# Another order of VectorE's instructions, and gathers released by free slots, in a graph network's edge loop

## The chip, the cores and the metric

One core of one Trainium2 chip. The metric is the device time of one execution in microseconds.

## The reference

A graph of 6250 nodes with 32 features and 106250 edges (`src`, `dst`, sorted by `dst`). Three layers of graph attention with 8 heads, each followed by a residual and a batch norm; then one message layer over the same edges. What one attention layer computes:

```python
xl = (x @ Wl + bl).reshape(n, H, C)
xr = (x @ Wr + br).reshape(n, H, C)
e = leaky_relu(xl[src] + xr[dst], 0.2)
logits = einsum('ehc,hc->eh', e, att)
m = segment_max(logits, dst)
p = exp(logits - m[dst])
denom = segment_sum(p, dst)
alpha = p / (denom[dst] + 1e-16)
out = segment_sum(xl[src] * alpha[:, :, None], dst).mean(axis=1) + bias
```

The message layer gathers features by `src`, forms a radial weight per edge, mixes, and adds the messages at `dst`.

## The kernel before, in words

Edges are laid out in steps of 256 (two to a partition), 480 steps a layer, so arranged that all edges of a step end in one block of 128 nodes; `brow` holds the block's number of each step. A layer is ten groups of 48 steps; a group is eight bodies of six steps (`S6`), the first and the last body written out, the six between them in a hardware loop on each engine. The layers and the groups 1 to 9 are hardware loops too.

A step k goes through the engines like this:

- GpSimd (L473 to L492) copies the indices of three steps (L478), then for each step issues two indirect gathers of the neighbours' rows (L490), 128 rows each, into slot k mod 6 of `xg`. Before a step it waits for `front_done` (L482) and `xs_done` (L483), that is until TensorE and ScalarE have read the slot's previous content, of step k-6. In addition the first gather waits for `oht_done` (L486), VectorE's one-hot of step k-3, and the second for `r_done` (L488), VectorE's reduction of step k-8. `then()` (L461) increments `passed`, which nobody waits for.
- SyncE loads the local destinations `dr`, three steps at a time (L410).
- VectorE makes a one-hot of the destinations (`one_hot_t`, L1139), five steps ahead. TensorE turns the gathered rows and adds the destination's rows (`front`, L597 and L600), four steps ahead; ScalarE copies the result to SBUF (`keep`, L807) and the plain rows to `xs` (L808), three steps ahead; TensorE makes the scores (`zed`, L609 and L611), two steps ahead, into one of two PSUM places; VectorE weights them (`weighted`, L1144) and reduces over channels (`over_channels`, L1152), and ScalarE copies the linear part (`linear`, L816). Every three steps VectorE writes logits (L1158).
- After a group its maxima per destination are found (`maxima`, one long chain over the engines, with L1277 near its end), and the logits are exponentiated.
- Beside group g, the weights of group g-1 are used: VectorE multiplies the rows by them (`weigh_rows`, L1171), TensorE sums over the edges with another one-hot from ScalarE (`aggregate`, L624), and VectorE adds the result to the accumulator of the step's block (`add_sums`, L1182), two steps later. For that it loads the block's number from `brow` into a register (L1178). The aggregation of k waits for the product of k and the sum of k-2 (L620, L622).

Group 0 has no aggregation beside it, and a last drain group (g = 10) has only the aggregation. A self-loop stage, the layer's output and the batch norm follow. After three layers comes the message layer (from L1383 for VectorE), which has a loop and gathers of its own (L513).

VectorE's order in a step is written out in `dve_body` (L1184): sum of k-2, product of k, logits where due, one-hot of k+5, weighting of k, reduction of k. The queues of an engine work in order; the semaphores count up over the whole kernel.

Of the kernel before, what the change touches and what calls it, by code (L numbers as in the profile page):

```python
# [38 lines left out]
S6 = 6  # L39
# [34 lines left out]
def gatv2_program(nc, x, src, dst, edge_w, edge_v, Wl, bl, Wr, br, att, conv_bias, gamma, beta,  # L74
# [3 lines left out]
    with ctx:  # L78
# [364 lines left out]
        def _(pool):  # L443
# [23 lines left out]
            with pool.Fori(0, LAYERS) as l:  # L467
# [5 lines left out]
                with pool.Fori(0, GROUPS) as g:  # L473
                    with pool.Fori(0, BODIES // 2) as i:
                        k0 = (g * BODIES + i * 2) * S6
                        for a in range(0, 2 * S6, 3):

                            nc.gpsimd.tensor_copy(idx[:, a:a + 3, :], srci[:, bass.ds(k0 + a, 3), :]).then_inc(idx_done, 1)  # L478
                            pool.wait_ge(idx_done, AHEAD + ((l * GROUPS + g) * BODIES + i * 2) * 2 + a // 3 + 1)
                            for s in range(a, a + 3):  # L480

                                pool.wait_ge(front_done, AHEAD + l * ZS + k0 + s + 1 - S6)  # L482
                                pool.wait_ge(xs_done, AHEAD + l * NS + k0 + s + 1 - S6)  # L483
                                for t in range(2):
                                    if t == 0:
                                        pool.wait_ge(oht_done, AHEAD + l * NS + k0 + s + 1 - 3)  # L486
                                    else:
                                        pool.wait_ge(r_done, AHEAD + l * ZS + k0 + s + 1 - 8)  # L488
                                    then()
                                    nc.gpsimd.indirect_dma_start(  # L490
                                        out=xg[:, s % S6, t, 96:128], out_offset=None, in_=table,
                                        in_offset=bass.IndirectOffsetOnAxis(ap=idx[:, s, t:t + 1], axis=0)).then_inc(gat[s % S6], 16)  # L492
# [481 lines left out]
        def _(v):  # L974
# [199 lines left out]
                    pg[:, 2 * j:2 * j + 2, bass.ds(c, 1), :].rearrange("p e o h -> p e (o h)").unsqueeze(3).to_broadcast([P, 2, H, C1]),  # L1174
                    ALU.mult).then_inc(px_done, 1)

            def add_sums(l, g, k, r):
                b = v.value_load(brow[0:1, bass.ds(k, 1)], min_val=0, max_val=BLOCKS - 1)  # L1178
                v.wait_ge(agg_done, AHEAD + l * NS + k + 1)
                v.wait_ge(acc_done, AHEAD + l * AGGS + 2 + g + k)  # L1180
                sums = acc[:, bass.ds(b, 1), :].rearrange("p o a -> p (o a)")
                op.tensor_tensor(sums, sums, agg_ps(r), ALU.add).then_inc(acc_done, 1)  # L1182

            def dve_body(l, g, i, a, b, starts_group, ends_group):  # L1184
                k0 = (g * BODIES + i) * S6
                for s in range(S6):
                    r = s % 2
                    if b and (s > 1 or not starts_group):
                        add_sums(l, g - 1, k0 - GS + s - 2, r)
                    if b:  # L1190
                        weigh_rows(l, g - 1, i, k0 - GS + s, s)
                    if a and s == J:
                        chunk_logits(l, g, i, 0)
                    if a and s == 0 and not starts_group:
                        chunk_logits(l, g, i - 1, 1)
                    if a and (s + 5 < S6 or not ends_group):
                        one_hot_t(l, g, i, k0 + s + 5, s + 5)
                    if a:
                        weighted(l, k0 + s, r)
                        over_channels(l, k0 + s, r, (g * BODIES + i) * 2 + s // J, s // J, s % J)  # L1200

            def dve_group(l, g, a, b):
# [4 lines left out]
                if a:  # L1207
                    chunk_logits(l, g, BODIES - 1, 1)
                if b:
                    add_sums(l, g - 1, g * GS - 2, 0)  # L1210
                    add_sums(l, g - 1, g * GS - 1, 1)

            def early_places(l, g, steps):
                for s in steps:
# [342 lines left out]
```

## Time and profile before

| | us |
|---|---|
| median of 3 runs | 9670.92 (9669.8 to 9671.51) |
| profiled execution | 9705.39 |
| its span, first to last instruction | 9703.5 |
| mean granted TensorE clock | 0.758 |

The profile is of one execution. Its page lists busy time by engine and the costliest groups of instructions; the timelines give start and duration of single instructions in us from the span's start, with the idle time of the engine before one and what ended it in brackets. DVE is VectorE, PE TensorE, ACT ScalarE, POOL GpSimd; a q behind the name is the engine's sequencer, which handles registers, loads and waits. "issue" as a releaser means that the engine waited for nothing the profile shows.

### The profile page before, as it was taken

The numbers are of one execution on the slowest core, as the hardware profiler recorded it, in microseconds if no ns is written. First come the engines' busy times: TensorE is split into PE (matmuls) and PEld (weight loads), VectorE is DVE, ScalarE is ACT, GpSimd is POOL, SyncE is SP. The second block draws the span as 40 slices with busy tenths as digits, with TensorE's granted clock in tenths as the row PEclk, the third lists the DMA queues.
The fourth block names the chain that finished last, engine by engine and source line by source line (L and its number), as shares of the span: only waits on it lengthen the run. The fifth ranks groups of instructions, "written<-read, shape, count | busy, mean of one in ns | idle before, by whom it ended". The sixth has DMA issues, their size and how long they took to land. (4 is left out here: it accounts for less than half of the span.)

```text
span 9703.5 us, 180857 instructions
## 1 busy us (share of the span) xinstructions
PE 6644.2 (68%) x27124; PEld 4815.8 (50%) x27125; DVE 7465.0 (77%) x15346; ACT 3973.6 (41%) x14623; POOL 5056.5 (52%) x5548
## 2 busy tenths in 40 slices
PE   1777777775577777775577777776466666666666
PEld 0454555544355555544355545554455555555555
DVE  6677777774577777774577777775699999999999
ACT  0344544451255444452144444443144444444443
POOL 2555555521555555530455555540366666666666
PEclk7898999895799899996689989997555555555555
DMA  2111111110111111110111111110000000000001
GB/s 87 31 31 27 28 28 29 28 14 0 32 29 32 26 28 29 29 20 0 27 28 28 31 27 28 29 26 0 22 17 17 18 17 17 17 17 18 17 17 17
DMA packets 219588, 234.03 MB, mean 24 GB/s; under 512 B 74765, under 2 KB 200718, under 8 KB 219150
## 3 DMA queue, kind: packets, MB, share of 16 engines
q1 hardware_dynamic: 95630, 166.18, 5.9%
q0 software_dynamic: 123776, 66.31, 5.7%
q14 instruction: 175, 1.43, 0.1%
q8 instruction: 7, 0.11, 0.0%
HBM read 219.39 MB, written 12.80 MB: 24 GB/s over the span
## 5 line engine op out<-in xcount | busy, mean ns | idle before, releaser
L490 POOL DMA_INDIRECT xg<-table,idx x2880 | 2916.2, 1013 | 2437.5 <-issue 1341.1
L624 PE MATMUL psum<-px,oh 128*128 128x272 f32 x5760 | 1750.4, 428 | 835.3 <-issue 320.8
L609 PE MATMUL psum<-wz,xt 128*128 x6072 | 1972.4, 419 | 187.6 <-ACT lin L816 94.6
L624 PEld LDWEIGHTS psum<-px,oh 128*128 128x128 f32 x5760 | 1012.2, 196 | 1310.7 <-issue 1020.8
L609 PEld LDWEIGHTS psum<-wz,xt 128*128 128x128 f32 x6072 | 1015.1, 204 | 693.8 <-issue 298.8
L513 POOL DMA_INDIRECT xg<-table,idx x960 | 933.9, 973 | 583.4 <-issue 149.2
L796 ACT ACTIVATE dist<-iota_f,ndloc 128x128 f32<-128x128 f32 x2880 | 998.7, 394 | 464.2 <-PE psum L624 179.7
L1171 DVE TENSOR_TENSOR px<-xs,pg 128x528 f32 (+1 forms) x1440 | 1024.4, 712 | 207.7 <-issue 169.4
L1182 DVE TENSOR_TENSOR acc<-acc,psum 128x272 f32 x1440 | 630.6, 438 | 684.7 <-issue 562.2
L1152 DVE TENSOR_REDUCE lr<-u 128x16 f32<-128x512 f32 x1518 | 1037.6, 686 | 124.6 <-DVE u L1144 83.4
L759 PE MATMUL psum<-acc,oh 128*128 128x32 f32 x1920 | 509.8, 406 | 896.5 <-DVE acc L1508 894.8
L751 PE MATMUL psum<-w2e,xt 65*128 65x256 f32 x1920 | 1086.9, 670 | 50.1 <-ACT xt L915 45.6
L1144 DVE SCALAR_TENSOR_TENSOR u<-psum,atts 128x512 f32<-128x512 f32 x1518 | 1040.7, 686 | 93.6 <-PE psum L611 69.2
L530 POOL TENSOR_TENSOR xs<-acc,xg 128x384 f32<-128x384 f32 x960 | 901.6, 963 | 278.5 <-ACT acc L945 137.6
L816 ACT COPY lin<-psum 128x16 f32<-128x16 f32 x1518 | 261.3, 172 | 1882.5 <-DVE u L1144 1490.5
L759 PEld LDWEIGHTS psum<-acc,oh 128*128 128x128 f32 x1920 | 445.5, 322 | 1036.9 <-DVE acc L1508 1003.2
L611 PE MATMUL psum<-bz,ones_b 96*128 x3036 | 881.6, 290 | 0.0
L597 PE MATMUL psum<-ident,xg 128*128 128x128 f32 x2880 | 607.8, 295 | 274.5 <-DMA xg<-table,idx 170.1
L936 ACT ACTIVATE dist<-iota_f,ndloc 128x128 f32<-128x128 f32 x960 | 333.0, 394 | 1046.4 <-PE psum L759 936.3
L752 PEld LDWEIGHTS psum<-w2e,xt 65*128 65x128 f32 x1920 | 646.9, 337 | 172.9
L807 ACT COPY xt<-psum 128x256 f32<-128x256 f32 x1440 | 536.3, 372 | 454.2 <-PE psum L600 192.9
L1139 DVE TENSOR_SCALAR oht<-dr,iota_p 128x256 bf16<-128x256 bf16 x1440 | 407.8, 286 | 389.7 <-PE psum L600 140.3
(270 smaller groups left out, 9880.3 us busy)
## 6 DMA issues: line engine op xcount, KB each, us to landing
dr<-dlocs SPq DMA_DIRECT2D x480, 192.0 KB
xg<-table,idx POOLq DMA_INDIRECT x3840
acc<-w_rows SPq DMA_DIRECT2D x160, 192.0 KB
fl<-flags SPq DMA_DIRECT2D x30, 576.2 KB
flags<-fl SPq DMA_DIRECT2D x10, 576.2 KB, 3.2
table<-xn SPq DMA_DIRECT2D x4, 784.0 KB, 3.6
xp<-keys SPq DMA_DIRECT2D x5, 385.0 KB, 4.4
u<-keys SPq DMA_DIRECT2D x5, 385.0 KB, 4.4
```

Source lines behind the costliest of these rows:

```text
L490: nc.gpsimd.indirect_dma_start(out=xg[:, s % S6, t, 96:128], out_offset=None, in_=table, in_offset=bass.IndirectOffsetOnAxis(ap=idx[:, s, ...
L513: nc.gpsimd.indirect_dma_start(out=xg[:, s, e, 96:128], out_offset=None, in_=table, in_offset=bass.IndirectOffsetOnAxis(ap=idx[:, s, e:e + ...
L530: last = nc.gpsimd.tensor_tensor(pb[:, r, e].rearrange("p (i u v) -> p i u v", i=3, v=8)[:, 0:n], rb[:, r, e].rearrange("p (u v) -> p u v" ...
L609: pe.matmul(out_z, xt[:, r, e * P:(e + 1) * P], wz[:, bass.ds(l, 1), :].rearrange("p o z -> p (o z)"), start=True, stop=False)
L611: last = pe.matmul(out_z, ones_b[:], bz[:, bass.ds(l, 1), :].rearrange("p o z -> p (o z)"), start=False, stop=True)
L624: last = pe.matmul(agg_ps(r), oh[:, r, e, :], px[:, r, e, :], start=(e == 0), stop=(e == 1))
L751: pe.matmul(z_ps(r, 0, HC)[:, e, :], rows, w2e[:, 0:HC], start=True, stop=True)
L759: last = pe.matmul(psum[:, 6 + r, 0:C], oh[:, r, e, :], msg[:, r, e, :], start=(e == 0), stop=(e == 1))
L796: last = op.activation(dist[:, e, :], iota_f[:], ACT.Abs, bias=ndloc[:, bass.ds(k, 1), e])
L1144: op.scalar_tensor_tensor(u[:, r], z_ps(r, 0, HC), 0.0, atts[:, bass.ds(l, 1), :].to_broadcast([P, 2, HC]), ALU.max, ALU.mult).then_inc(u_ ...
L1152: op.tensor_reduce(lr[:, c, j], u[:, r].rearrange("p e (h c) -> p e h c", h=H), AX.X, ALU.add).then_inc(r_done, 1)
L1171: op.tensor_tensor(px[:, r, :, 0:H * C1].rearrange("p e (h c) -> p e h c", h=H), rows.unsqueeze(2).to_broadcast([P, 2, H, C1]), pg[:, 2 * ...
```

## The change

VectorE: in each step the product of k now stands ahead of the sum of k-2. The block's number is no longer loaded inside `add_sums` but by `block_at`. In a body that also weighs edges it is loaded a step ahead, between the weighting and the reduction of the step before, and kept in a register; in the first step of a body (in a group's first body, in the first step that adds) it is loaded on the spot, as in the drain group and at a group's end.

GpSimd: the waits for `oht_done` and `r_done` are gone. A step's two gathers are issued as a pair, once the slot is free; `passed` is incremented once a step, not twice.

```diff
--- before.py
+++ after.py
@@ -481,12 +481,8 @@
 
                                 pool.wait_ge(front_done, AHEAD + l * ZS + k0 + s + 1 - S6)
                                 pool.wait_ge(xs_done, AHEAD + l * NS + k0 + s + 1 - S6)
+                                then()
                                 for t in range(2):
-                                    if t == 0:
-                                        pool.wait_ge(oht_done, AHEAD + l * NS + k0 + s + 1 - 3)
-                                    else:
-                                        pool.wait_ge(r_done, AHEAD + l * ZS + k0 + s + 1 - 8)
-                                    then()
                                     nc.gpsimd.indirect_dma_start(
                                         out=xg[:, s % S6, t, 96:128], out_offset=None, in_=table,
                                         in_offset=bass.IndirectOffsetOnAxis(ap=idx[:, s, t:t + 1], axis=0)).then_inc(gat[s % S6], 16)
@@ -1174,8 +1170,11 @@
                     pg[:, 2 * j:2 * j + 2, bass.ds(c, 1), :].rearrange("p e o h -> p e (o h)").unsqueeze(3).to_broadcast([P, 2, H, C1]),
                     ALU.mult).then_inc(px_done, 1)
 
-            def add_sums(l, g, k, r):
-                b = v.value_load(brow[0:1, bass.ds(k, 1)], min_val=0, max_val=BLOCKS - 1)
+            def block_at(k):
+                return v.value_load(brow[0:1, bass.ds(k, 1)], min_val=0, max_val=BLOCKS - 1)
+
+            def add_sums(l, g, k, r, b):
+
                 v.wait_ge(agg_done, AHEAD + l * NS + k + 1)
                 v.wait_ge(acc_done, AHEAD + l * AGGS + 2 + g + k)
                 sums = acc[:, bass.ds(b, 1), :].rearrange("p o a -> p (o a)")
@@ -1185,10 +1184,13 @@
                 k0 = (g * BODIES + i) * S6
                 for s in range(S6):
                     r = s % 2
-                    if b and (s > 1 or not starts_group):
-                        add_sums(l, g - 1, k0 - GS + s - 2, r)
+                    adds = b and (s > 1 or not starts_group)
                     if b:
                         weigh_rows(l, g - 1, i, k0 - GS + s, s)
+                    if adds and not a:
+                        add_sums(l, g - 1, k0 - GS + s - 2, r, block_at(k0 - GS + s - 2))
+                    if adds and a:
+                        add_sums(l, g - 1, k0 - GS + s - 2, r, block_at(k0 - GS + s - 2) if s == 0 or (starts_group and s == 2) else ahead)
                     if a and s == J:
                         chunk_logits(l, g, i, 0)
                     if a and s == 0 and not starts_group:
@@ -1197,6 +1199,9 @@
                         one_hot_t(l, g, i, k0 + s + 5, s + 5)
                     if a:
                         weighted(l, k0 + s, r)
+                    if b and a and s + 1 < S6 and (s > 1 or not starts_group):
+                        ahead = block_at(k0 - GS + s - 1)
+                    if a:
                         over_channels(l, k0 + s, r, (g * BODIES + i) * 2 + s // J, s // J, s % J)
 
             def dve_group(l, g, a, b):
@@ -1207,8 +1212,8 @@
                 if a:
                     chunk_logits(l, g, BODIES - 1, 1)
                 if b:
-                    add_sums(l, g - 1, g * GS - 2, 0)
-                    add_sums(l, g - 1, g * GS - 1, 1)
+                    add_sums(l, g - 1, g * GS - 2, 0, block_at(g * GS - 2))
+                    add_sums(l, g - 1, g * GS - 1, 1, block_at(g * GS - 1))
 
             def early_places(l, g, steps):
                 for s in steps:
```

## Rows read from the trace of the kernel before

**Rows 1.** Page, busy time, share of the span and instructions of each engine.

```profile
PE 6644.2 (68%) x27124; PEld 4815.8 (50%) x27125; DVE 7465.0 (77%) x15346; ACT 3973.6 (41%) x14623; POOL 5056.5 (52%) x5548
```

**Rows 2.** L1277 (once between two groups), from 580 to 780 us, one line's instructions.

```profile
L1277 DVE TENSOR_TENSOR acc<-acc,fixn x2: 433/434/435, 587.9 to 775.3; 128x264 f32 x2
```

**Rows 3.** Timeline of VectorE around the end of a body: start, duration, engine, line.

```profile
1069.76 0.44 DVE L1182 TENSOR_TENSOR acc<-acc,psum 128x272 f32 x1 [0.79 <-issue]
...
1089.04 0.69 DVE L1152 TENSOR_REDUCE lr<-u 128x16 f32<-128x512 f32 x1
1090.50 0.44 DVE L1182 TENSOR_TENSOR acc<-acc,psum 128x272 f32 x1 [0.77 <-issue]
1091.10 0.71 DVE L1171 TENSOR_TENSOR px<-xs,pg 128x528 f32 x1 [0.16 <-issue]
```

**Rows 4.** Timeline of VectorE, one step inside a body and the next sum.

```profile
1053.10 0.44 DVE L1182 TENSOR_TENSOR acc<-acc,psum 128x272 f32 x1 [0.38 <-issue]
1053.69 0.71 DVE L1171 TENSOR_TENSOR px<-xs,pg 128x528 f32 x1 [0.16 <-issue]
1054.32 0.28 DVE L1139 TENSOR_SCALAR oht<-dr,iota_p 128x256 bf16<-128x256 bf16 x1
1054.51 0.68 DVE L1144 SCALAR_TENSOR_TENSOR u<-psum,atts 128x512 f32<-128x512 f32 x1
1055.23 0.69 DVE L1152 TENSOR_REDUCE lr<-u 128x16 f32<-128x512 f32 x1
1056.29 0.44 DVE L1182 TENSOR_TENSOR acc<-acc,psum 128x272 f32 x1 [0.38 <-issue]
```

**Rows 5.** L1178, the load of the block's number, from 404 to 590 us.

```profile
L1178 DVEq TENSOR_LOAD <-brow x48: 298/305/327, 407.6 to 567.2; - x48
```

**Rows 6.** Timeline of TensorE, two aggregations in a row.

```profile
1057.79 1.18 PE L624 MATMUL psum<-px,oh 128*128 128x272 f32 x4 [0.56 <-DVE px L1171]
...
1060.99 0.49 PE L624 MATMUL psum<-px,oh 128*128 128x272 f32 x1 [0.56 <-DVE px L1171]
```

**Rows 7.** Timeline of GpSimd in group 0 of the first layer.

```profile
337.61 0.95 POOL L490 DMA_INDIRECT xg<-table,idx  x1 [0.30 <-issue]
...
339.77 1.02 POOL L490 DMA_INDIRECT xg<-table,idx  x1 [1.00 <-PE psum L600]
...
342.35 0.96 POOL L490 DMA_INDIRECT xg<-table,idx  x1 [0.30 <-issue]
```

**Rows 8.** Timeline of VectorE in the last stage, a reduction and what follows.

```profile
8003.39 0.69 DVE L1473 TENSOR_REDUCE acc<-u 128x32 f32<-128x512 f32 x1
8003.99 0.19 DVE L1448 TENSOR_REDUCE acc<-xp 128x16 f32<-128x48 f32 x1
```

**Rows 9.** Timeline of VectorE in the drain group, product, sum, product.

```profile
2121.62 0.71 DVE L1171 TENSOR_TENSOR px<-xs,pg 128x528 f32 x1
2122.68 0.44 DVE L1182 TENSOR_TENSOR acc<-acc,psum 128x272 f32 x1 [0.34 <-issue]
2123.19 0.71 DVE L1171 TENSOR_TENSOR px<-xs,pg 128x528 f32 x1
```

**Rows 10.** Page, costliest groups: the gathers (busy, mean ns | idle, releaser).

```profile
L490 POOL DMA_INDIRECT xg<-table,idx x2880 | 2916.2, 1013 | 2437.5 <-issue 1341.1
```

**Rows 11.** L490, the gathers of group 0, from 235 to 380 us.

```profile
L490 POOL DMA_INDIRECT xg<-table,idx x90: 949/955/1020, 235.7 to 375.5; - x90
```

**Rows 12.** Timeline of all engines, a product and a gather behind it.

```profile
1087.50 0.71 DVE L1171 TENSOR_TENSOR px<-xs,pg 128x528 f32 x1
1087.55 1.49 POOL L490 DMA_INDIRECT xg<-table,idx  x1 [0.30 <-issue]
```

**Rows 13.** L1171 and L1139, all instances: duration ns minimum, median, maximum.

```profile
L1171 DVE TENSOR_TENSOR px<-xs,pg x1440: 697/708/783, 403.6 to 6632.3; 128x528 f32 x150, 128x528 f32<-128x528 f32 x30
...
L1139 DVE TENSOR_SCALAR oht<-dr,iota_p x1440: 275/281/523, 218.2 to 6522.1; 128x256 bf16<-128x256 bf16 x180
```

**Rows 14.** L1443, the last stage's product of two SBUF inputs, 7900 to 8100 us.

```profile
L1443 DVE TENSOR_TENSOR xp<-xg,acc x36: 192/789/2381, 7900.9 to 8098.1; 128x48 f32<-128x48 f32 x36
```

## The prediction, made before the change was run

> **What bounds the kernel now.** I read the page first. The span is 9703.5 us; VectorE is busy for 77% of it, TensorE for 68%, GpSimd for 52% [rows 1], averages over stages with different limits. The change touches only the edge stage, so I went to its timelines, engine by engine. A layer runs ten groups of 48 steps that weigh edges; in groups 1 to 9 each step also aggregates a step of the group before. From one correction of the carried maximum to the next a whole group takes 187.4 us [rows 2]. The steps alone: one pass through the six-step body takes from 1069.76 to 1090.50, that is 20.74 us, 3.46 a step [rows 3]; 27 such groups of 48 are 1296 steps.
>
> Inside a body a step is 3.19 us from one sum on VectorE to the next [rows 4]. VectorE waits there twice: 0.38 us before the sum and 0.16 before the rows' product. No other engine is named; the releaser is issue. So VectorE's own sequencer is what is late. It takes things in order: the block's number is loaded in 0.305 us [rows 5], and turned into an address, before the sum that uses it can start. TensorE starts its aggregation every 3.20 us and stood idle 0.56 of that, waiting for the product [rows 6]: it needs 2.64. GpSimd I read in group 0, where there is nothing to aggregate: a gather takes 0.96 after an idle 0.30, so 1.26 us from start to start, and after every sixth the next one starts 2.16 later, because a copy of indices and its wait lie between [rows 7]. Three steps cost it 5 x 1.26 + 2.16 = 8.46, 2.82 a step. So VectorE sets the pace of a step, and behind it stand GpSimd at 2.82 and TensorE at 2.64.
>
> **VectorE's order.** Today's step is five links, start to start [rows 4]: reduction to sum 1.06 (0.69 of work, then the load's tail), sum to product 0.59, product to one-hot 0.63, one-hot to weighting 0.19, weighting to reduction 0.72. Sum 3.19. In the new order:
> - Reduction to product: the reduction's own length, 0.69, or a little less, since the next instruction overlaps its end; a 0.69 reduction of the last stage let the next start after 0.60 [rows 8]. The product's register work takes up to the 0.59 seen between sum and product. I take 0.60.
> - Product to sum: no load between, so the product's own 0.63. Sum to one-hot: the sum lasts 0.44; with the same overlap of 0.08 as the product it is 0.36. I take 0.40.
> - One-hot to weighting 0.19, as now.
> - Weighting to reduction: the load now stands here. If the sequencer goes on while the weighting runs, as it does today while the reduction runs, load, address and check fit under the 0.72 that the reduction waits anyway for the weighting. The bounds come from the drain group, where the load stands between a product and a sum: start to start 1.06 [rows 9], and that includes the sum's register work, about 0.3, so 0.72 to 1.06. I take 0.72, because the reduction has hardly any register work of its own.
> The step comes to 0.60 + 0.63 + 0.40 + 0.19 + 0.72 = 2.54, 0.65 less; with the load uncovered 2.88, 0.31 less.
>
> The first step of a body keeps its load on the spot. Today it runs reduction, 1.46, sum, 0.60, product [rows 3], and 0.63 on from there as in [rows 4]. Afterwards: reduction to product about 1.0 (1.46 less the load's 1.06, plus 0.60), product to sum 1.06 as in the drain group, sum onward 0.40: 2.46 against 2.69, about 0.2 less. A body of VectorE alone becomes 20.74 - 5 x 0.65 - 0.2 = 17.3 us. The number of loads stays, so does the number of sums; the drain group runs product, load, sum in a circle of 1.57 us before [rows 9] and after, nothing gained.
>
> What this moves past: the sum of step k-2 now comes behind the product of k. TensorE's aggregation waits for both; today the product is last, afterwards the sum, 0.40 after the product's effective end. TensorE then starts later within the step, but its own circle of 2.64 x 6 = 15.8 us a body stays under 17.3. By the code its scores (zed, L605 to L613) run two steps ahead of the weighting that reads them, and the sum reads an aggregation of two steps before, which covers the shift; without that cover it would cost up to 0.40 a step. No wait is added on any engine; behind the sum stand the one-hot and the weighting, and ScalarE's copy at L816 waits for the weighting, which moves with the step.
>
> **The gathers.** Removed are two waits a step on GpSimd's queue, for the one-hot of k-3 and the reduction of k-8 (L486, L488), and one of two increments of `passed`, which nobody waits for. What is left is the slot's own release: front and copy of rows of k-6. No gather is added. What becomes possible is that GpSimd keeps going; what is late next is its own pace. Its free pace is 8.46 x 2 = 16.9 a body. On top comes stretching: a gather lasts 955 ns by the median, in group 0 never over 1020, but 1013 in the mean of all, and 1.49 us when it starts just behind the product [rows 10 to 12]. In the mean that is 0.06 a gather, 0.12 a step now. Freed from VectorE's pace the gathers start anywhere in the step: with the bad part the product's first 0.45 of 2.8 us (an estimate; at most its whole 0.71), times two gathers, times up to 0.5, it is 0.15 a step. So 2.82 + 0.15 = 2.97, a body of 17.8, and this, not VectorE's 17.3, is the likeliest bound. It can be somewhat better, since with six slots GpSimd can start a group several steps ahead, and worse, if it stops at the edges.
>
> **Sum.** 20.74 - 17.8 = 2.9 us a body. 27 groups of 8 bodies are 216; the first body of each group adds only three preloaded sums, so I count 7.4 a group, 200 bodies: 580 us. Group 0 of each layer, now 3.14 a step by its gathers' starts (139.8 us for 89 intervals of half a step [rows 11]), may gain from a sixth slot, 0 to 6 us a layer; I count nothing. The profiled execution took 9705.4 us, 1.9 outside its span, and gives 9125; it stands 34 above the median of 9670.9, so on the median's footing I predict 9095.
>
> **A rule against it.** The product is never longer than 783 ns and the one-hot's median is 281 against a least of 275 [rows 13], though gathers run beside both: the trace shows gathers giving way, never VectorE. The page "SBUF — State Buffer" of the Trainium skill, section "Who interferes with whom", states that VectorE and GpSimd share one pair of ports as an exclusive lock and that issue order decides who blocks. The stretched gather agrees with it; a VectorE stopped by gathers in this stage is the half that no row shows.
>
> **The rivals.**
> 1. The load isn't hidden behind the weighting (or the pace falls only to group 0's 3.14 a step). Then 3.46 goes to 3.14 by either way: 0.32 x 1296 steps = 415 us, 9255. For it: the sequencer is in order, and in group 0 GpSimd, with little to wait for, is that slow [rows 11]. Against: weighting to reduction has 0.72 of cover.
> 2. VectorE's 17.3 is reached, as GpSimd uses its head start: 3.4 x 200 = 680, 8990.
> 3. Slower: gathers no longer timed by VectorE stop VectorE. In the last stage its small product of two SBUF inputs takes 192 to 2381 ns beside GpSimd's products [rows 14]. If product and one-hot both had to wait for a gather under way (1.91 of every 2.54 us, half of 0.96 each), that is 2 x 0.36 = 0.72 a step, more than the 0.65 gained: 0.07 x 1296 = 90 us slower, 9760. It decides from 0.65 a step on. Against: [rows 13].
> 4. Gathers stop the one-hot alone: 0.36 x 1296 = 465 of the 680 in rival 2 go back, 9455. Against: the one-hot's durations [rows 13] and a product-to-one-hot distance of 0.63 with a gather running, as without. This is what the lock on the Trainium skill's page "SBUF — State Buffer" would do where the gather came first.
> 5. It changes nothing, since something the profile doesn't name holds 3.4 a step. The issue gaps speak against it.
>
> **Chances.** Forecast, within 60 us: 0.45; rival 2: 0.2; rival 1 and values between: 0.22; rival 3: 0.06; rival 4: 0.03; rival 5: 0.04. The range takes the first three with their bounds, 2.9 to 3.2 a step (0.56 and 0.26 x 1296 off 9671): 8950 to 9330. A measurement of this kernel tells 0.2% from no change. Faster 0.91, same 0.03, slower 0.06.
>
> **What would show it.** Idle before the sum (L1182's successor) falls from 0.38 to about 0 in five of six steps, and weighting to reduction stays 0.72; were it 1.06, rival 1. GpSimd's idle before gathers falls to 0.30 with few waits for anybody, and its mean gather rises a little over 1013 ns. A product or one-hot longer than today, or idle before the one-hot, would be rival 3 or 4. TensorE waiting for gathers in the fronts would say that GpSimd is the bound. The forecast is wrong if the body stays over 19.5 us.

## The result, and the profile after

The changed kernel took 9813.19 us (median of 4 runs, 9795.74 to 9834.9) beside 9671.22 for the kernel before on the same chip: ratio 1.0148, 95% interval 1.0127 to 1.0168. That is 1.5% slower, where 6% faster was forecast. The experiments below show that the sign differs from chip to chip. On two of the five chips used for experiments the kernel before takes about 9495 us; on one of them the same change was measured and takes 0.9333 of that. On the three others, as on the first, the kernel before takes 9668 to 9705 us; on two of them the same change was measured, and it is slower. I call them prompt and late chips, for a reason that the traces give.

The page of the changed kernel, busy time and TensorE's clock over the span (9793.9 us; the line numbers up to VectorE's part are 4 lower than before, the sum is now L1181):

```profile
PE 6747.0 (69%) x27124; PEld 5039.5 (51%) x27125; DVE 7371.9 (75%) x15346; ACT 3854.4 (39%) x14623; POOL 4971.5 (51%) x5548
...
PEclk7788888895688888887688888888555555555555
...
L486 POOL DMA_INDIRECT xg<-table,idx x2880 | 2853.1, 991 | 2619.1 <-ACT xs L804 1348.7
L605 PE MATMUL psum<-wz,xt 128*128 x6072 | 2099.2, 441 | 773.8 <-ACT lin L812 668.9
```

Against [rows 1] VectorE is busy for 93 us less (7465.0 to 7371.9) in a span that is 90 longer, and GpSimd for 85 less: its gathers last 991 ns in the mean, not 1013 [rows 10]. Only TensorE is busy for longer, by 103 us in matmuls, at a granted clock that fell from 0.758 to 0.727; VectorE and GpSimd wait more. The gathers' largest wait used to be their own issue; now it is ScalarE's copy of the rows, 1348.7 us: GpSimd runs ahead until all slots are full, and for that time it is not what holds the step.

The timeline of VectorE after, first a step as forecast, then steps that are not:

```profile
442.90 0.28 DVE L1135 TENSOR_SCALAR oht<-dr,iota_p 128x256 bf16<-128x256 bf16 x1
443.09 0.68 DVE L1140 SCALAR_TENSOR_TENSOR u<-psum,atts 128x512 f32<-128x512 f32 x1
443.81 0.69 DVE L1148 TENSOR_REDUCE lr<-u 128x16 f32<-128x512 f32 x1
444.42 0.70 DVE L1167 TENSOR_TENSOR px<-xs,pg 128x528 f32 x1
445.03 0.43 DVE L1181 TENSOR_TENSOR acc<-acc,psum 128x272 f32 x1
445.38 0.28 DVE L1135 TENSOR_SCALAR oht<-dr,iota_p 128x256 bf16<-128x256 bf16 x1
...
451.43 0.30 DVE L1135 TENSOR_SCALAR oht<-dr,iota_p 128x256 bf16<-128x256 bf16 x1 [2.17 <-PE psum L596]
...
457.70 0.32 DVE L1135 TENSOR_SCALAR oht<-dr,iota_p 128x256 bf16<-128x256 bf16 x1 [0.87 <-PE psum L596]
```

One-hot to one-hot is 2.48 us (442.90 to 445.38), with links of 0.19, 0.72, 0.61, 0.61 and 0.35: the new order does what was forecast at 2.54, and the load is hidden. But then the one-hot waits 2.17 and 0.87 us for a front (L596) on TensorE. The timeline of TensorE and its waiters in one such place:

```profile
525.62 0.27 PE L596 MATMUL psum<-oht,x 128*96 128x256 bf16 x1
...
525.73 1.08 PE L620 MATMUL psum<-px,oh 128*128 128x272 f32 x4
...
528.42 0.30 PE L596 MATMUL psum<-oht,x 128*96 128x256 bf16 x1 [0.26 <-issue]
...
528.84 1.18 PE L620 MATMUL psum<-px,oh 128*128 128x272 f32 x4
529.22 0.29 DVE L1135 TENSOR_SCALAR oht<-dr,iota_p 128x256 bf16<-128x256 bf16 x1 [2.72 <-PE psum L596]
...
531.57 0.69 ACT L792 ACTIVATE dist<-iota_f,ndloc 128x128 f32<-128x128 f32 x2 [4.03 <-PE psum L620]
531.78 0.71 DVE L1167 TENSOR_TENSOR px<-xs,pg 128x528 f32 x1 [0.65 <-remote]
```

The front of 525.62 ends at 525.89 by its row, and who waits for it starts at 529.22. The aggregation of 525.73 ends at 526.81, and ScalarE starts at 531.57. The semaphore events of the trace say the same (an increment is the event by which an instruction signals that it is done): the front's increment stands at 529.20, and then four increments of TensorE (aggregation, scores, front, aggregation) stand between 531.44 and 531.65, though the work that they report fills more than 2 us. The first of them is that of the aggregation of 525.73, 4.6 us late. These are the **late completions**: who waits goes on when TensorE's signal is seen, not when the profile lets its matmul end. In groups 1 to 9 of this trace 50 of 100 scores have an increment within 0.05 us of their modelled end (58 before).

That share mixes two things, late increments and increments that the trace doesn't hold. The traces of late chips lack many, of every engine: of the 1296 scores in groups 1 to 9 this trace holds 1159 increments (1057 before, all 1296 in run 7 below), of VectorE's 1518 weightings 1134 (run 7: 1517), and of the gathers' 61696 increments 29704 (run 7: 61029). Of the recorded increments of the scores 56 of 100 are on time here and 71 before; of the aggregations 41 here and 93 before. Of VectorE's and ScalarE's recorded increments all but 18 of 17029 stand within 0.02 us of the end; only TensorE's are seen late. Every time here has a granted clock beside it, so it seems that each execution was recorded too; whether the recording has a part in the delay, no run shows.

TensorE's clock follows. Windows of 6 us: length, busy time of each engine, granted clock, share of DMA, GB/s:

```profile
498.00:504.00 6.00, 5.37 (x28) 4.17 (x29) 5.55 (x13) 4.00 (x17) 3.21 (x4) 1.00 0.04 5
504.00:510.00 6.00, 2.73 (x13) 1.52 (x11) 2.77 (x6) 1.83 (x8) 2.72 (x4) 1.00 0.25 44
510.00:516.00 6.00, 5.90 (x24) 4.62 (x25) 4.83 (x10) 3.65 (x16) 3.89 (x4) 0.72 0.07 8
...
528.00:534.00 6.00, 2.63 (x9) 1.45 (x8) 3.82 (x8) 2.36 (x9) 2.10 (x3) 0.77 0.18 41
534.00:540.00 6.00, 6.00 (x24) 4.71 (x23) 4.03 (x9) 2.85 (x13) 3.82 (x4) 0.67 0.08 11
```

TensorE works 2.6 to 2.7 of 6 us where signals are late, and part of the next stretch runs at 1.2 GHz, the lower of its two levels (granted clock 0.72 and 0.67 over the 6 us), where it is busy nearly all the time with 24 matmuls instead of the 28 of the first stretch.

### The profile page after: what moved, and what is told of

The parts are those of the page before. It is cut to its first block and busy times, and to the rows that moved or that the text cites. A ratio compares the mean times of both kernels' runs of the same rounds, so it can differ in the third digit from the quotient of the medians.

```text
span 9793.9 us, 177731 instructions
## 1 busy us (share of the span) xinstructions
PE 6747.0 (69%) x27124; PEld 5039.5 (51%) x27125; DVE 7371.9 (75%) x15346; ACT 3854.4 (39%) x14623; POOL 4971.5 (51%) x5548
## 5 line engine op out<-in xcount | busy, mean ns | idle before, releaser
L486 POOL DMA_INDIRECT xg<-table,idx x2880 | 2853.1, 991 | 2619.1 <-ACT xs L804 1348.7
L605 PE MATMUL psum<-wz,xt 128*128 x6072 | 2099.2, 441 | 773.8 <-ACT lin L812 668.9
L620 PE MATMUL psum<-px,oh 128*128 128x272 f32 x5760 | 1792.4, 438 | 147.7 <-DVE acc L1181 77.4
L605 PEld LDWEIGHTS psum<-wz,xt 128*128 128x128 f32 x6072 | 1138.1, 217 | 1268.3 <-issue 546.5
L620 PEld LDWEIGHTS psum<-px,oh 128*128 128x128 f32 x5760 | 1086.5, 210 | 465.0 <-DVE acc L1181 178.7
L509 POOL DMA_INDIRECT xg<-table,idx x960 | 930.8, 970 | 583.4 <-issue 150.3
L607 PE MATMUL psum<-bz,ones_b 96*128 x3036 | 918.8, 303 | 0.0
L593 PE MATMUL psum<-ident,xg 128*128 128x128 f32 x2880 | 647.3, 311 | 317.3 <-DMA xg<-table,idx 171.2
L1181 DVE TENSOR_TENSOR acc<-acc,psum 128x272 f32 x1440 | 622.7, 432 | 202.3 <-issue 154.9
L593 PEld LDWEIGHTS psum<-ident,xg 128*128 128x128 f32 x2880 | 407.7, 160 | 567.8 <-issue 266.8
```

Of the source, the lines that this page charges most:

```text
L486: nc.gpsimd.indirect_dma_start(out=xg[:, s % S6, t, 96:128], out_offset=None, in_=table, in_offset=bass.IndirectOffsetOnAxis(ap=idx[:, s, ...
L509: nc.gpsimd.indirect_dma_start(out=xg[:, s, e, 96:128], out_offset=None, in_=table, in_offset=bass.IndirectOffsetOnAxis(ap=idx[:, s, e:e + ...
L593: pe.transpose(xt_ps(r)[:, e * P:(e + 1) * P], xg[:, s, e, :], ident[:])
L605: pe.matmul(out_z, xt[:, r, e * P:(e + 1) * P], wz[:, bass.ds(l, 1), :].rearrange("p o z -> p (o z)"), start=True, stop=False)
L607: last = pe.matmul(out_z, ones_b[:], bz[:, bass.ds(l, 1), :].rearrange("p o z -> p (o z)"), start=False, stop=True)
L620: last = pe.matmul(agg_ps(r), oh[:, r, e, :], px[:, r, e, :], start=(e == 0), stop=(e == 1))
```

## The experiments

Times are medians; each ratio is to the kernel before on the same chip, with its 95% interval.

| run | kernel | chip | before, us | this, us | ratio | granted clock |
|---|---|---|---|---|---|---|
| 7 | whole change | prompt | 9493.16 | 8859.48 | 0.9333 (0.9317 to 0.9349) | 0.757 |
| 1 | order alone | prompt | 9495.75 | 8886.42 | 0.9359 (0.9343 to 0.9375) | 0.754 |
| 8 | order alone | prompt | 9493.16 | 8881.91 | 0.9358 (0.9342 to 0.9373) | 0.755 |
| 4 | sum first, load ahead | prompt | 9495.75 | 8899.89 | 0.9374 (0.9359 to 0.939) | 0.756 |
| 3 | product first, load on the spot | prompt | 9495.75 | 9285.85 | 0.9777 (0.9761 to 0.9794) | 0.766 |
| 2 | gathers alone | prompt | 9495.75 | 9482.99 | 0.9987 (0.9977 to 0.9996) | 0.765 |
| 9 | gathers alone | prompt | 9493.16 | 9479.77 | 0.9986 (0.9977 to 0.9996) | 0.767 |
| 5 | whole change | late | 9673.02 | 9805.27 | 1.0148 (1.0122 to 1.0175) | 0.728 |
| 14 | whole change | late | 9667.98 | 9815.98 | 1.0137 (1.0106 to 1.0168) | 0.728 |
| 15 | order alone | late | 9667.98 | 9588.17 | 0.992 (0.9904 to 0.9937) | 0.734 |
| 10 | order alone | late | 9705.41 | 9677.37 | 0.9971 (0.996 to 0.9983) | 0.730 |
| 11 | sum first, load ahead | late | 9705.41 | 9622.01 | 0.9916 (0.9899 to 0.9932) | 0.728 |
| 12 | product first, load on the spot | late | 9705.41 | 9608.74 | 0.9899 (0.9882 to 0.9915) | 0.754 |
| 13 | gathers alone | late | 9705.41 | 9747.89 | 1.0044 (1.0028 to 1.0059) | 0.752 |
| 16 | order, one gather a step | late | 9667.98 | 8689.39 | 0.8987 (0.8972 to 0.9002) | 0.756 |
| 17 | order, places to one partition | late | 9667.98 | 9584.8 | 0.9918 (0.9902 to 0.9935) | 0.732 |
| 18 | order, second gather 4 bytes a row | prompt | 9491.17 | 8859.59 | 0.9336 (0.9321 to 0.9352) | 0.755 |

Run 6, the kernel before once more on the chip of run 5, gave 9675.76. Runs 1 to 4 and 18 share a chip, so do runs 5 and 6, 7 to 9, 10 to 13, and 14 to 17. Run 18 came 42 minutes after runs 1 to 4, and the kernel before took 9491.17 there where it had taken 9495.75: the level stayed with the chip.

**Runs 1 to 4: the parts, each alone.** The order alone keeps GpSimd's waits for `oht_done` and `r_done` (the first hunk of the diff is left out); the gathers alone is that hunk and nothing else.

```diff
 # run 3: product first, load on the spot
-                        add_sums(l, g - 1, k0 - GS + s - 2, r, block_at(...) if s == 0 or (...) else ahead)
+                        add_sums(l, g - 1, k0 - GS + s - 2, r, block_at(k0 - GS + s - 2))
-                    if b and a and s + 1 < S6 and (s > 1 or not starts_group):
-                        ahead = block_at(k0 - GS + s - 1)
 # run 4: the sum (number loaded a step ahead) stands before weigh_rows, as in the kernel before
```

Run 1, the order alone:

> VectorE's new order with the gathers released by VectorE as before. Theory clock: the new order lets TensorE run densely for a few steps and then wait, the granted clock falls some eight times in a group of 165 us (34 us at 1.2 GHz in the changed kernel, 9 in the kernel before), and each fall costs what the order saves. Then this kernel alone is at 9750 to 9850 us with a mean clock near 0.73. Rival gathers: the free-running gathers are what makes TensorE's completions late and the clock fall; then this kernel keeps a clock near 0.76 and is faster than before, by up to the 0.6 us a step that the steps without a stall show (2.48 against 3.19), 9000 to 9400.

Run 2, the gathers alone:

> The gathers released by free slots, VectorE's order as before. Theory clock: VectorE still sets an even pace of 3.2 us, TensorE waits a little in each step, the clock stays: 9640 to 9680 us, clock near 0.758. Rival gathers: 9800 or more, with a clock near 0.73 and more falls of it in a group.

Run 3, product first:

> Product ahead of the sum, the block's number loaded on the spot between them, gathers as before. A step of VectorE alone is then 0.60 + 1.06 + 0.40 + 0.19 + 0.72 = 2.97 against 3.19, so 0.2 us a step of 1296 steps, 280 us at most. Theory clock: TensorE's need leaves little idle; if the clock holds, 9400 to 9600; if it falls as in the changed kernel, 9700 or more. Rival gathers: faster, 9400 to 9500.

Run 4, load ahead:

> Sum first as before, its block's number loaded a step ahead, gathers as before. A step of VectorE alone: reduction to sum 0.60, sum to product 0.59, product to one-hot 0.63, 0.19, 0.72 = 2.73 against 3.19, up to 0.46 a step. TensorE's aggregation waits for the product as before. Theory clock: somewhere between, 9500 to 9800, with a clock under 0.758. Rival gathers: 9200 to 9350 with the clock kept.

The order alone brought 6.4% and the gathers 0.13%: each part by itself gained, and together they had lost. Of the order, the load ahead is what pays (0.9374 against 0.9359 with the product's new place on top); the product's place alone brings 2.2%, and next to nothing once the load is ahead. But the kernel before took 9495.75 here and not 9671, so two readings stood: the parts spoil each other, or this was another kind of chip.

**Runs 5 and 6: the whole change again, and the kernel before.** Both kernels are unchanged.

> The whole change once more, beside the kernel before on the same chip. In the first pair of profiles TensorE's completions came up to some us after the modelled end of its matmuls in both kernels; in the four single parts they came at once, and the kernel before took 9496 us there, not 9671. Theory surroundings: the late completions belong to the chip of the first comparison and not to the change; then this run is at 8860 to 8960 us, 6% under the kernel before on this chip. Rival interaction: order and gathers are harmless alone and harmful together; then it is at 1.01 to 1.02 of the kernel before, 9590 to 9690, with a clock near 0.73.

> The kernel before, for its profile on this chip. Theory surroundings: TensorE's completions come at the modelled ends (over 95% of them), group 0 takes about 125 us instead of 150, the steps of groups 1 to 9 about 156 instead of 161, the time is 9496 within 15 us. Rival interaction: the profile looks like the one shown before, group 0 at 150 us.

The whole change gave 1.0148 once more, beside a kernel before of 9673.02. The loss repeats, and it came again with the slower kernel before, so the readings were still not told apart.

**Runs 7 to 9: whole, order and gathers side by side.** The kernels are those of the whole change and of runs 1 and 2; all three share a chip.

> The whole change beside its two parts on one chip. So far the parts ran on one chip (kernel before 9496 us, TensorE's completions at once), the whole on others (9671 us, completions late). Theory chip: which of the two a chip is decides. Where the kernel before takes about 9496 us, the whole takes 8860 to 8960; where it takes about 9671, it takes about 9805 again. Rival interaction: 1.01 to 1.02 of the kernel before on either.

> VectorE's order alone, on the same chip as the run before this one. Theory chip: on a chip with late completions this is not at 0.936 of the kernel before but at 0.98 to 1.02, its clock falling many times in a group; on a chip without, 0.936 again. Rival interaction: 0.936 on either.

> The gathers alone. Theory chip: within 0.5% of the kernel before, on either kind of chip, since VectorE's order still sets the pace. Rival interaction: the same. A third reading, that free-running gathers are what delays TensorE's completions: 1.01 or more on a chip with late completions.

These were made on a prompt chip. The whole change takes 0.9333, better than the order alone by 0.3%. That refutes the reading in which the parts spoil each other wherever they meet. The timeline of VectorE in run 7, the whole change on a prompt chip:

```profile
447.57 0.70 DVE L1167 TENSOR_TENSOR px<-xs,pg 128x528 f32 x1
448.19 0.43 DVE L1181 TENSOR_TENSOR acc<-acc,psum 128x272 f32 x1
448.54 0.28 DVE L1135 TENSOR_SCALAR oht<-dr,iota_p 128x256 bf16<-128x256 bf16 x1
448.74 0.68 DVE L1140 SCALAR_TENSOR_TENSOR u<-psum,atts 128x512 f32<-128x512 f32 x1
449.45 0.69 DVE L1148 TENSOR_REDUCE lr<-u 128x16 f32<-128x512 f32 x1
450.52 0.71 DVE L1167 TENSOR_TENSOR px<-xs,pg 128x528 f32 x1 [0.38 <-ACT xs L804]
451.58 0.44 DVE L1181 TENSOR_TENSOR acc<-acc,psum 128x272 f32 x1 [0.35 <-issue]
...
467.39 0.71 DVE L1167 TENSOR_TENSOR px<-xs,pg 128x528 f32 x1 [0.38 <-ACT xs L804]
```

A body is 467.39 - 450.52 = 16.87 us, where the forecast had 17.3 for VectorE alone, and no step of it waits for a front. TensorE's matmuls fill 16.06 us of this body. The waits of the two traces of one and the same kernel (engine, line, whom it waited for: us in total, times, longest), first on the late chip:

```profile
POOL xg L486 <- ACT xs L804: 1348.7, 477, 13.6
ACT dist L792 <- PE psum L620: 1056.1, 710, 4.6
...
PE psum L605 <- ACT lin L812: 668.9, 282, 4.5
```

and run 7, on the prompt one:

```profile
POOL xg L486 <- ACT xs L804: 513.4, 276, 12.8
...
ACT dist L792 <- PE psum L620: 357.4, 540, 5.4
```

ScalarE waits 699 us less for the aggregations (L620), GpSimd 835 less for ScalarE's copies. In run 7's trace every scores' signal of groups 1 to 9 comes within 0.05 us of its modelled end (1.00, against 0.50). The kernel, its code and its data are the same: the late completions are a property of the chip, or of what else was on it; no run tells which.

**Runs 10 to 13: the parts on a late chip.** The same kernels as in runs 1, 4, 3 and 2.

> The order alone a third time, for a chip on which the kernel before takes about 9672 instead of 9495 us. If the chip is again of the 9495 kind: 0.936. If it is of the 9672 kind, theory A (the late completions of TensorE stop any VectorE order that runs at 2.5 us a step): 1.00 to 1.02, as the whole change (1.0148), with steps of groups 1 to 9 over 155 us and over 600 us at 1.2 GHz. Theory B (there it is the freed gathers that turn the gain into a loss): 0.93 to 0.95, as on the other chips.

> Sum first, number loaded a step ahead, gathers as before. On a chip of the 9495 kind 0.937 again. On one of the 9672 kind, theory A: between 0.99 and 1.02, as the order alone, since its step is as short. A rival: the aggregation is needed last here (the product comes behind the sum, so TensorE waits for it as before), and that leaves the completions more slack: 0.96 to 0.98.

> Product first, number loaded on the spot, gathers as before: a step of 3.15 us on the 9495 kind (0.978 again). On one of the 9672 kind, theory A: the step is slow enough for late completions to be mostly hidden, so it keeps a gain, 0.975 to 0.99, and is faster there than the order alone. Theory B: 0.978, slower than the order alone.

> The gathers' change alone, old order. On a chip of the 9495 kind 0.9986. On one of the 9672 kind, theory A: 0.995 to 1.003, it does nothing there either. Theory B: 1.01 or more.

Here every order lands close to the kernel before: 0.9971, 0.9916, 0.9899, where the prompt chip had 0.936, 0.937 and 0.978. It is no longer VectorE's step that counts: over groups 1 to 9 a step (from the starts of the weighting) takes 3.40, 3.37 and 3.37 us, where the prompt chips have 2.85, 2.86 and 3.17, and the kernel before 3.43 on the first chip. The gathers alone cost 0.4%. Theory A's numbers held for load ahead and, at their edge, for the product first; the order alone came a little below its 1.00, and the gathers alone a little above its 1.003. Theory B, that only the freed gathers spoil the gain, is refuted by run 10. Whether the clock has a part in that floor isn't settled. Run 12 has 0.754 and run 11 0.728, with 0.1% between their times, which speaks against the clock as the whole cause. But between 400 and 6600 us TensorE stands at 1.2 GHz for 2024 us in run 10 and 2027 in run 11, and for 1544 in run 12 and 1502 before: the two shorter orders may pay in clock what they save in work, and no run separates the late signal from the clock that falls after it.

**Runs 14 to 17: which transfer does it.** Run 14 is the whole change and run 15 the order alone, for comparison. Run 16 leaves the second gather of each step out of the order alone (half of the source rows of the attention are then zero), run 17 cuts SyncE's load of the places from 128 partitions to one and sets the others to zero once at the start (their one-hots are then wrong).

```diff
 # run 16
                                 for t in range(2):
...
-                                    nc.gpsimd.indirect_dma_start(
+                                    if t == 0:
+                                        nc.gpsimd.indirect_dma_start(
...
-                pe.wait_ge(gat[s], 32 * t + 32)
+                pe.wait_ge(gat[s], 16 * t + 16)
 # run 17
-                    sp.dma_start(dr[:, 3 * half:3 * half + 3, :]...
-                                 dlocs[...].partition_broadcast(P)).then_inc(drl[half], 16)
+                    sp.dma_start(dr[0:1, 3 * half:3 * half + 3, :]...
+                                 dlocs[...].partition_broadcast(1)).then_inc(drl[half], 16)
```

> The whole change beside the order alone on one chip. Where the kernel before takes about 9495: 0.933. Where it takes 9670 to 9705: 1.015 again, so that against the order alone (0.997) the freed gathers cost 1.5 to 2 per cent more; a rival is that they cost 0.4 per cent as on the old order, and that the chips differ for the rest: 1.00.

> The order alone as the base of the two next runs: 0.936 on a chip of the 9495 kind, 0.997 on one of the other.

> The order alone with one gather a step instead of two (the second half of every step's source rows is left out of the attention, so the output differs). On a chip of the 9495 kind GpSimd is not what holds a step, so within 0.5 per cent of the order alone. On a chip of the other kind, if the late completions come from the traffic of the gathers or of their descriptors: at least 3 per cent below the order alone, most completions on time. If the gathers have nothing to do with them: within 1 per cent of it.

> The order alone with SyncE's load of the places (768 numbers broadcast to 128 partitions) cut to one partition (the output differs). These loads run only in groups 0 to 9, as the late completions do. If they cause them: at least 3 per cent below the order alone on a chip of the 9670 to 9705 kind. If not: within 1 per cent. On a chip of the 9495 kind within 0.5 per cent of the order alone.

They ran on a late chip. The whole change beside the order alone is 9815.98 / 9588.17 = 1.024: with the short step the freed gathers cost 2.4%, not the 0.4% of run 13. With one gather a step the kernel takes 8689.39, below anything on a prompt chip; the scores' signals of groups 1 to 9 are on time again (1.00 within 0.05 us, against 0.44 in run 15; of the recorded increments 1.00 against 0.55). With the places cut down nothing changes. So **the late completions come with the gathers**, and not with what SyncE's loads write.

Gathers alone aren't enough, though: how close they follow seems to count. In the message layer of the trace after, 960 gathers start 2.82 us apart in the mean (7047.6 to 9750.6), and of the signals that TensorE gives there, two kinds, 480 each, 478 and 340 are recorded and all but one of each kind are on time. Run 16 has one gather per 2.81 us in groups 1 to 9, on time, and one per 1.8 us in group 0, where 0.74 of the recorded scores' signals are on time. Two gathers a step are one per 1.6 to 1.7 us in run 15. No run changes the distance by itself.

The weighting's instances of group 0 and group 1, 48 steps each (duration min, median, max; first and last start). Run 15, two gathers, late chip:

```profile
L1144 DVE SCALAR_TENSOR_TENSOR u<-psum,atts x48: 677/691/693, 236.6 to 382.6; 128x512 f32<-128x512 f32 x48
L1144 DVE SCALAR_TENSOR_TENSOR u<-psum,atts x48: 678/687/693, 404.2 to 560.7; 128x512 f32<-128x512 f32 x48
```

Run 16, one gather, the same chip:

```profile
L1145 DVE SCALAR_TENSOR_TENSOR u<-psum,atts x48: 676/685/692, 231.2 to 315.7; 128x512 f32<-128x512 f32 x48
L1145 DVE SCALAR_TENSOR_TENSOR u<-psum,atts x48: 678/685/693, 336.8 to 469.3; 128x512 f32<-128x512 f32 x48
```

Run 7, two gathers, prompt chip:

```profile
L1140 DVE SCALAR_TENSOR_TENSOR u<-psum,atts x48: 680/691/693, 236.0 to 361.1; 128x512 f32<-128x512 f32 x48
L1140 DVE SCALAR_TENSOR_TENSOR u<-psum,atts x48: 675/683/693, 382.2 to 514.9; 128x512 f32<-128x512 f32 x48
```

Group 1 takes 132.5 us with one gather on the late chip and 132.7 with two on the prompt one, so the second gather doesn't set the pace there, and VectorE does, at 2.82 a step; with two on the late chip it is 156.5, 3.33 a step. Group 0, which has no aggregation, is held by the gathers: 146.0 us on the late chip and, with one, 84.5. The 125.1 of the prompt chip shows that late signals lengthen it too. Of the 899 us between runs 15 and 16, 3 x 61.5 = 185 are group 0's, which any chip would give in part; taking group 1 for all, 27 x 24.0 = 648 lie in groups 1 to 9.

**Run 18: number or bytes.** The order alone; the second gather keeps its 128 rows, but fetches 4 bytes of each instead of 128 (its half of the source rows is wrong).

```diff
-                                        out=xg[:, s % S6, t, 96:128], out_offset=None, in_=table,
+                                        out=xg[:, s % S6, t, 96:128 if t == 0 else 97], out_offset=None,
+                                        in_=table if t == 0 else table.rearrange("r (c o) -> (r c) o", o=1),
```

> The order alone with the second gather of each step kept as an instruction, with its 128 descriptors, but fetching 4 bytes a row instead of 128 (its half of the source rows is wrong, so the output differs). On a chip of the 9495 kind: as the order alone, 0.936, which tells nothing more. On one of the other kind (the order alone 0.992 to 0.997, one gather a step 0.899): if it is the bytes of the gathers that delay TensorE's completions, 0.90 to 0.94; if it is the number of gathers or of their descriptors, 0.98 to 1.00.

It ran on a prompt chip, 0.9336, and tells nothing of late completions there; 0.2% under runs 1 and 8 is all that the bytes cost there. Whether bytes, descriptors or the gather's instruction delays TensorE's signals on a late chip stays open.

## Why the prediction was wrong

What failed is what it said of TensorE ("What this moves past"), and nothing of VectorE's order; GpSimd as the bound was wrong as well, by 0.9 us a body (17.8 against 16.87). Point by point:

**The new step, 2.54.** Right: 2.48 measured on both kinds of chip, in steps where nothing is late; the load fits under the weighting (rival 1 fell). The body came out at 16.87 against 17.3.

**"What this moves past", TensorE.** This is the step that failed. I gave TensorE a circle of 2.64 a step, 15.8 us a body, from the matmuls' modelled ends, and concluded that it stays under 17.3. On the chip that was profiled, the signal of its work came 1 to 5 us late in many steps. In the kernel before these delays were there too (29 of 100 recorded scores' signals, but only 7 of 100 aggregations'):

```profile
1160.69 0.27 PE L600 MATMUL psum<-oht,x 128*96 128x256 bf16 x1
...
1160.80 1.08 PE L624 MATMUL psum<-px,oh 128*128 128x272 f32 x4
...
1162.45 0.28 DVE L1139 TENSOR_SCALAR oht<-dr,iota_p 128x256 bf16<-128x256 bf16 x1 [0.56 <-PE psum L600]
...
1163.40 0.69 ACT L796 ACTIVATE dist<-iota_f,ndloc 128x128 f32<-128x128 f32 x2 [2.02 <-PE psum L624]
```

The front ends at 1160.96 by its row and the aggregation at 1161.88; who waits for them starts at 1162.45 and 1163.40. The long step of before seems to have hidden most of it, which is argued from the times: the kernel before is 1.9% slower on late chips (9671 against 9495), the order alone 7.9 to 8.9% (9588.17 and 9677.37 against 8886.42). A step of 2.5 us has no such slack, and 3.35 to 3.40 us a step is what is left, near the 3.43 of before. That comes nearest to rival 5, "something the profile doesn't name holds 3.4 a step", to which I gave 0.04 and which forecast no change, not a loss. Its sign stood in the trace of before, as the rows above show. The views that I read (busy time, groups, VectorE's timeline) follow VectorE; the waits for TensorE of ScalarE and of the fronts' readers, laid against the modelled end of what they waited for, could have shown it.

**GpSimd as the bound, 17.8 a body.** Wrong on both kinds of chip. On prompt chips the order alone and the whole change differ by 0.3%, and with one gather a step group 1 is no shorter. A gather's mean fell to 991 ns (993 in run 7) instead of rising over 1013: the term for stretching, 0.15 us a step, measured 0.08 (two gathers, each 0.04 over the median). Without it my own 8.46 us for three steps [rows 7] give 16.9 a body, and in run 7 two copies of indices with their six gathers each take 450.27 to 467.29, 17.0, beside VectorE's 16.87: the two engines' paces are about equal there. That GpSimd has head start as well, 1348.7 us of waiting for free slots show. What was argued as rival 2, VectorE's own pace, is what prompt chips show.

**The gathers' part, no wait added.** True of the code, and on prompt chips it brings 0.13% alone and 0.3% with the order. On late chips it costs 0.4% alone and 2.4% on top of the order. There fewer of TensorE's signals are on time: of the recorded increments of the aggregations 58 of 100 with the order alone (run 15) and 41 with the whole change (run 14, the same chip). Why was not tried; that gathers come closer together after each late signal, when several slots come free at once, is argued, not shown.

**Rivals 3 and 4, gathers stopping VectorE.** The result is on rival 3's side of zero, but it isn't its mechanism. The product and the one-hot in the trace after (ns min, median, max; first and last start):

```profile
L1167 DVE TENSOR_TENSOR px<-xs,pg x1440: 696/707/803, 403.4 to 6727.4; 128x528 f32 x150, 128x528 f32<-128x528 f32 x30
```

```profile
L1135 DVE TENSOR_SCALAR oht<-dr,iota_p x1440: 272/285/537, 219.7 to 6619.4; 128x256 bf16<-128x256 bf16 x180
```

Against 708 and 783, 281 and 523 [rows 13] neither waits inside itself for a gather. The lock of which the Trainium skill's page "SBUF — State Buffer", section "Who interferes with whom", speaks shows here on GpSimd's side alone, as the forecast had it.

**The sum.** 200 bodies by 2.9 gave 580 us. On prompt chips the whole change saves 9493.16 - 8859.48 = 634, between the forecast's 580 and rival 2's 680; from the gathers alone to the whole change it is 9479.77 - 8859.48 = 620. The terms don't count the 0.13% of the gathers, and the body before is shorter there than the 20.74 of the profiled chip: a step of groups 1 to 9 takes 3.32 us with the gathers alone (run 2), not 3.43. That the size comes out near 580 is in part luck, since the bound behind it was the wrong one. On the median's footing the sum was also added up 4 us too high: 9125 less 34 is 9091, not 9095. On late chips the same sum is worth 28 to 80 us without the gathers, and minus 132 to 148 with them. The range and the chances were made for one chip's behaviour; that the chip itself could differ, I hadn't put in.

**Which version to keep.** No version tried wins most on both. The order without the gathers' change has 0.936 on prompt and 0.992 to 0.997 on late chips, and sum first with the load ahead 0.937 and 0.992: either is faster on both, and the gathers' change is worth 0.3% on one kind against 2.4% on the other.

## What to carry to other kernels

A dependency ends when its signal is seen: before you count an engine's slack from the modelled ends of its matmuls, lay the start of whoever waited against that end, in several places of the trace, and take the later one. When a step is shortened, ask which delay the long step had been hiding, and put the time of the unchanged kernel beside every ratio: two values of it, 9495 and 9670 here, are two machines, and a change has to be measured on both. Before you count the events of a trace, count how many it should hold. Releasing transfers as early as possible wasn't free here: it cost 2.4% on late chips once the step was short.

## What the runs showed of the hardware

- The same kernel has two levels, by chip: 9491 to 9496 us in the prompt runs, 9668 to 9705 in the late ones. The difference seen is in TensorE's signals, which on late chips arrive microseconds after the modelled end (4.6 for the aggregation of 525.73 above), several at once. They are late in the groups of the attention in which gathers run; in the drain group, the self-loop stage and the message layer the recorded ones are on time, and with half of the gathers left out those of groups 1 to 9 are too (run 16). That the signals wait and not the matmuls is read from the bunch of 0.21 us, and what holds them is open.
- A gather that starts 0.05 to 0.1 us behind VectorE's product of two SBUF operands lasts longer: 1.49 us in [rows 12], 1.47 in the median of 186 such gathers before, where the median of all of group 0's is 0.955 [rows 11]. Started 0.2 to 0.3 us behind, it lasts 1.30 (69 gathers). The product stays at 0.71.
- Group 0, from the first weighting's start to the last, takes 125.1 us with two gathers a step on a prompt chip and 143.7 to 150 on late ones; with one, on a late chip, 84.5.
